# Counts before ranks, and comparisons in half precision, at the end of a routing stage

## The chip, the core and the metric

The kernel runs on one core of one Trainium2 chip. The metric is the device time of one execution in microseconds; before the change it is 438.07 us, the median of 3 runs (436.51 to 440.91). A core has five engines that run their own instruction streams and meet at semaphores: TensorE (PE, matmuls), VectorE (DVE), ScalarE (ACT), GpSimd (POOL) and SyncE (SP, which here only issues DMAs). PE's clock has two levels, 1.2 and 2.4 GHz, and the profile shows which was granted.

## The reference

A block of a transformer with two gated parts. `x` has 4 x 1024 rows of 256; the context has 77 rows of 256 for each of the 4 sequences.

```
h  = layernorm(x)
s  = h @ ctx^T / 16,  masked where query and key are both past the length
x1 = x + tanh(g_x) * (softmax(s) @ ctx @ W^T + b)

h2      = layernorm(x1)
routing = softmax(h2 @ router^T)              # 8 experts
top 2 of 8, their weights normalised to sum 1
y_e     = (silu(h2 @ Wg_e^T) * (h2 @ Wu_e^T)) @ Wd_e^T      # hidden 512
out     = x1 + tanh(g_f) * sum over the 2 chosen experts of weight * y_e
```

Each of the 4096 rows goes to 2 of 8 experts, so there are 8192 (row, expert) entries. The kernel computes an expert only for the rows that chose it.

## The kernel before, in words

**Stage one** (to about 100 us) goes over the rows in 8 groups of 512 (GROUPS = 8, 4 tiles of 128 rows each). Per group: scores, softmax and attention on PE, ACT and DVE; the row sums; the router's logits; then on DVE the two largest of 8 logits for each row and their one-hot form `oh` (L903). POOL adds the two to `picks` (L464), keeps running counts per expert (`carry`), normalises the rows and writes them with their 8 combining weights to `pay`. SP stores `pay` to `xn_rows` in HBM (L333), 512 rows at a time, and also the sums to the output, and between these it issues the loads of the experts' weights `raw` (L327), all in one queue and in order.

**The list.** The second stage needs, for each expert, the list of its rows, padded to whole pairs of 128-row tiles: 78 columns (TILES) of 128 places, 39 pairs (PAIRS). It is built without sorting. PE gives each entry its rank within its expert by products with a triangular matrix (`ranks`, L1112 to L1116), and the counts of all experts (L1151, L1153). A unit is one choice of one tile, so there are 64 units (UNITS) of 128 entries, 8 (CU) for a group. For an entry, the low 7 bits of its rank say the place within a column, and the start of its expert plus the high bits say the column. DVE writes two one-hot forms for each unit: `at_low` (L801, 128 x 128 in float16, which also carries the row's number), and `at_tile` (L949, the column's one-hot form, 78 wide, done for 16 units (CHUNK) in one comparison). PE then adds `at_low[u]^T @ at_tile[u]` over the 64 units (L1163), and the result is the list. Five small steps of DVE (L955 to L963) turn it into `idx`.

**The end of stage one on DVE** (function around L903 to L949), in order: oh of the last group; at_low of the group before, 8 units; the share of the last group; its ranks (po, rank), their low and high bits (low_i, high, low); then, once PE has the counts, nti, nts, ntf, cum, start (the rounded counts and their running sum), starts (start times oh, over all 64 units), first (its sum over 8 experts), col (first plus high). Each of these eight waits for the one before it, and one at_low of the last group stands behind each as a filler. Then four comparisons for at_tile. `mark` adds a semaphore step to an instruction and `after` waits for it.

**PE meanwhile** runs products that nobody reads (`keep_busy`, L1030: 128 x 512 in bfloat16, 22 of them before the counts, 18 behind the ranks and 22 behind the list).

**Stage two** takes the pairs in order. POOL gathers the 2 x 128 rows of a pair by `idx` from `xn_rows` (L495), four pairs ahead; before the first gather it waits for idx, for all stores of `xn_rows` and of the sums. PE transposes them (L1213 for the first pair, L1173 later), ACT and DVE cut them into a high and a low part (`xtT`), and three products stand for one in float32: gate and up (L1182), then down (L1203). ACT and DVE cut the weights of the next pair the same way (`gu`, `dn`). POOL adds the results to the output (L503). SP waits for the first gathers before it loads experts 4 to 7.

Of the kernel before, what the change touches and what calls it, by code (L numbers as in the profile page):

```python
# [14 lines left out]
P = 128  # L15
# [40 lines left out]
def moe_flamingo(nc, x, xT, ctx_rows, ctxT, lens, g_x, g_f, w_rows, wT, b_row, b_col, router, weights, out):  # L56
# [3 lines left out]
    with es:  # L60
        def sb(name, shape, dt=F32, stack=es):
            return stack.enter_context(nc.sbuf_tensor(name, shape, dt))
# [4 lines left out]
        def sem(name):  # L67
            return es.enter_context(nc.semaphore(name))
# [39 lines left out]
        iota_t = sb("iota_t", [P, TILES], F16, a)  # L108
# [25 lines left out]
        oh = sb("oh", [P, GROUPS, TOPK, G, NE], F32, a)  # L134
# [15 lines left out]
        starts = sb("starts", [P, UNITS, NE], F32, a)  # L150
        first = sb("first", [P, UNITS], F32, a)
        col = sb("col", [P, UNITS], F32, a)
# [9 lines left out]
        start = sb("start", [P, NE], F32, a)  # L162
# [6 lines left out]
        at_tile = sb("at_tile", [P, UNITS, TILES], F16, a)  # L169
# [71 lines left out]
        counts_ready = sem("counts_ready")  # L241
        tile_hot = sem("tile_hot")
# [164 lines left out]
        def _(pool):  # L407
# [30 lines left out]
            gp.iota(iota_t[:], [[1, TILES]], base=0, channel_multiplier=0, **exact)  # L438
# [3 lines left out]
            gp.dma_start(out[N:N + P, :], pad_tile[:, 0:D]).then_inc(y_added, Y_ADDED0)  # L442
            pool.wait_ge(gates_ready, 1)
# [248 lines left out]
        def _(dve):  # L692
# [18 lines left out]
            def mark(ins):  # L711
                steps[0] += 1
                ins.then_inc(dve_steps, 1)
                return steps[0]
# [55 lines left out]
            def share(k):  # L770
                dve.wait_ge(gap_sum_ready, k + 1)
                v.reciprocal(rw[:], ed1[:]).then_inc(share_ready, 1)
# [21 lines left out]
            def at_lows(k, units):  # L794

                if k < 0:
                    return
                dve.wait_ge(places_ready, k + 1)
                for u in units:
                    n = k * G + u % G  # L800
                    last = ts(at_low[:, k * CU + u], iota_p[:], low[:, k * CU + u:k * CU + u + 1], code[:, n:n + 1],  # L801
                              ALU.is_equal, ALU.mult)
                if u == CU - 1:
                    last.then_inc(low_ready, 1)
# [34 lines left out]
            for k in range(GROUPS):  # L839
# [66 lines left out]
                if more:  # L906
                    inverted = reciprocal_sums(n)
                elif k == GROUPS - 1:
                    at_lows(k - 1, range(CU))
                if k < 2:  # L910
                    values(k + 2)

            last_group = GROUPS - 1
            share(last_group)
            dve.wait_ge(chosen, GROUPS)
            ranked = unit_ranks(last_group, own_ranks(last_group))
# [3 lines left out]
            dve.wait_ge(counts_ready, 1)  # L920
            counted = mark(ts(nti[:], L[:, COUNTS:COUNTS + NE], float(PT - 1), None, ALU.add))
            at_lows(last_group, range(0, 1))
            after(counted)

            counted = mark(ts(nts[:], nti[:], PT.bit_length() - 1, 1, ALU.logical_shift_right, ALU.logical_shift_left))
            at_lows(last_group, range(1, 2))
            after(counted)
            counted = mark(v.tensor_copy(ntf[:], nts[:]))
            at_lows(last_group, range(2, 3))
            after(counted)  # L930
            counted = mark(v.tensor_tensor_scan(cum[:], one8[:], ntf[:], 0.0, ALU.mult, ALU.add))
            at_lows(last_group, range(3, 4))
            after(counted)
            begun = mark(tt(out=start[:], in0=cum[:], in1=ntf[:], op=ALU.subtract))
            at_lows(last_group, range(4, 5))
            after(begun)
            begun = mark(tt(out=starts[:], in0=oh[:].rearrange("p g c t e -> p (g c t) e"),
                            in1=start[:].unsqueeze(1).to_broadcast([P, UNITS, NE]), op=ALU.mult))
            at_lows(last_group, range(5, 6))
            after(begun)  # L940
            begun = mark(v.tensor_reduce(first[:], starts[:], axis=AX.X, op=ALU.add))
            at_lows(last_group, range(6, 7))
            after(begun)
            after(high_bits)
            begun = mark(tt(out=col[:], in0=first[:], in1=high[:], op=ALU.add))
            at_lows(last_group, range(7, 8))
            after(begun)
            for c in range(0, UNITS, CHUNK):
                tt(out=at_tile[:, c:c + CHUNK], in0=iota_t[:].unsqueeze(1).to_broadcast([P, CHUNK, TILES]),  # L949
                   in1=col[:, c:c + CHUNK].unsqueeze(2).to_broadcast([P, CHUNK, TILES]),  # L950
                   op=ALU.is_equal).then_inc(tile_hot, 1)
# [72 lines left out]
        def _(pe):  # L1024
# [133 lines left out]
            for u in range(UNITS):  # L1158
                if u % CHUNK == 0:
                    pe.wait_ge(tile_hot, u // CHUNK + 1)  # L1160
                if u % CU == 0:
                    pe.wait_ge(low_ready, u // CU + 1)
                last = mm(L[:, LIST:LIST + TILES], at_low[:, u], at_tile[:, u], start=(u == 0), stop=(u == UNITS - 1))  # L1163
            last.then_inc(list_ready, 1)
            keep_busy(22)
# [48 lines left out]
            last.then_inc(xT_ready, 1)  # L1214
            pe.wait_ge(x_low, 1)
# [59 lines left out]
```

## Time and profile before

| | before |
|---|---|
| median of 3 runs | 438.07 us |
| lowest, highest | 436.51, 440.91 us |
| the profiled execution's own time | 438.52 us |
| its span in the trace | 436.7 us |
| PE busy | 413.7 us, 95% |
| DVE busy | 314.8 us, 72% |
| ACT busy | 285.4 us, 65% |
| POOL busy | 251.4 us, 58% |
| mean granted PE clock | 0.979 |

The span is what the trace covers; the execution's time is 1.8 us more. PE's share of busy time is high in part because the unread products count as work. The profile divides the span into 40 slices of 10.9 us; the slice in tenths of each engine:

```profile
PE   8999889967899999999999999999999999999991
DVE  4448999994476777767767777777776777777771
POOL 5015446434236665766676665676667676567664
PEclk9999999988799999999999999999999999999997
```

Each digit is a tenth of full; PEclk is the granted clock. Slices 9 to 11 (87 to 120 us) are the passage from stage one to stage two, which the change is about.

### The profile page before, as it was taken

What the parts mean: (1) busy time and instruction counts of PE and PEld (TensorE: products, weight loads), DVE (VectorE), ACT (ScalarE), POOL (GpSimd) and SP (SyncE); (2) the same over time, 40 slices, a digit from 0 to 9 for tenths busy, and PEclk for the clock granted to TensorE, in tenths of its full rate; (3) what the DMA queues carried; (4) which work ended last, traced back from release to release, by engine and by line L of the source; (5) the groups of instructions that cost most, each with busy time, mean ns of one, the idle gap of its engine ahead of it and who ended that gap; (6) DMA issues with size and microseconds to landing.
All of it is one profiled execution on the core that took longest, in us unless ns stands there. A gap on an engine that the chain in (4) does not pass through costs nothing.

```text
span 436.7 us, 9843 instructions
## 1 busy us (share of the span) xinstructions
PE 413.7 (95%) x3237; PEld 378.9 (87%) x3237; DVE 314.8 (72%) x707; ACT 285.4 (65%) x581; POOL 251.4 (58%) x271
## 2 busy tenths in 40 slices
PE   8999889967899999999999999999999999999991
PEld 3778665534799999999999999999999999999991
DVE  4448999994476777767767777777776777777771
ACT  2698786302377767677676776767767677676770
POOL 5015446434236665766676665676667676567664
PEclk9999999988799999999999999999999999999997
DMA  6956866777457775434333343333433334333343
GB/s 196 328 181 210 267 211 207 248 245 235 109 141 162 162 162 138 67 59 69 50 56 57 59 72 49 54 58 60 66 55 53 56 61 68 55 52 58 63 64 65
DMA packets 34720, 50.52 MB, mean 116 GB/s; under 512 B 3878, under 2 KB 26055, under 8 KB 34695
## 3 DMA queue, kind: packets, MB, share of 16 engines
q0 software_dynamic: 13536, 19.46, 27.2%
q1 hardware_dynamic: 19815, 29.84, 22.2%
q10 hardware_dynamic: 1344, 0.92, 0.7%
q8 instruction: 11, 0.18, 0.2%
q14 instruction: 14, 0.11, 0.1%
HBM read 32.51 MB, written 17.70 MB: 115 GB/s over the span
## 4 chain that ended last, share of the span: by engine, by line
PE 75%; DVE 7%; DMA 7%; ACT 4%; issue 3%; POOL 2%; ACTq 1%; POOLq 0%; DVEq 0%
PE GT L1182 21%; PE Y L1203 20%; PE UP L1182 20%; DMA out_rows<-y,idx 4%; PE W L1030 3%; PE XT L1173 3%; DMA brow<-in_b_row 2%; DVE at_low L801 2%; PE O L1105 2%; ACT ex L582 2%; PE S L1055 2%; POOL xt L495 1%; DVE at_tile L949 1%; ACTq L538 1%; DMA xt<-xn_rows,idx 1%
## 5 line engine op out<-in xcount | busy, mean ns | idle before, releaser
L503 POOL DMA_INDIRECT out_rows<-y,idx x68 | 114.3, 1681 | 97.3 <-ACT y L654 66.6
L973 DVE TENSOR_TENSOR gu<-raw,gu 128x1024 fp32r<-128x1024 f32 x70 | 85.8, 1226 | 65.1 <-ACT gu L630 62.3
L1182 PE MATMUL GT<-xtT,gu 128*128 128x256 f32 x828 | 114.5, 288 | 2.6 <-DVE xtT L973 1.4
L495 POOL DMA_INDIRECT xt<-xn_rows,idx x76 | 97.1, 1277 | 33.7 <-issue 22.9
L1182 PE MATMUL UP<-xtT,gu 128*128 128x256 f32 x828 | 111.2, 284 | 0.0
L1182 PEld LDWEIGHTS GT<-xtT,gu 128*128 128x128 f32 x828 | 104.7, 193 | 4.6 <-DVE xtT L973 1.8
L1182 PEld LDWEIGHTS UP<-xtT,gu 128*128 128x128 f32 x828 | 105.0, 193 | 0.0
L1203 PE MATMUL Y<-dn,hT 128*128 128x256 f32 x816 | 103.5, 283 | 0.0
L1203 PEld LDWEIGHTS Y<-dn,hT 128*128 128x128 f32 x816 | 100.4, 192 | 0.0
L630 ACT CAST gu<-raw 128x1024 fp32r x68 | 70.8, 1042 | 34.3 <-PE UP L1182 31.9
L994 DVE TENSOR_TENSOR hid<-hid,UP 128x512 f32<-128x512 f32 x68 | 46.5, 684 | 9.3 <-PE UP L1182 9.0
L638 ACT CAST xtT<-XT 128x512 fp32r<-128x512 f32 x36 | 21.1, 587 | 42.4 <-issue 25.6
L973 DVE TENSOR_TENSOR hT<-hid,hT 128x512 fp32r<-128x512 f32 x68 | 46.6, 685 | 0.8
L643 ACT ACTIVATE hid<-GT 128x512 f32<-128x512 f32 x69 | 41.0, 594 | 9.0 <-PE GT L1182 7.4
L1030 PE MATMUL W<-ones 128*128 128x512 bf16 x180 | 44.0, 395 | 1.1 <-POOL ones L410 1.1
L647 ACT CAST hT<-hid 128x512 fp32r<-128x512 f32 x68 | 42.1, 619 | 3.8 <-DVE hid L994 2.3
L973 DVE TENSOR_TENSOR dn<-raw,dn 128x1024 fp32r<-128x1024 f32 x35 | 42.7, 1219 | 0.1
L654 ACT ACTIVATE y<-Y,xt 128x256 f32<-128x256 f32 x68 | 32.3, 475 | 6.3 <-PE Y L1203 5.4
L1030 PEld LDWEIGHTS W<-ones 128*128 128x128 bf16 x180 | 17.9, 102 | 21.3 <-issue 3.3
L634 ACT CAST dn<-raw 128x1024 fp32r x34 | 35.6, 1048 | 0.0
L973 DVE TENSOR_TENSOR xtT<-XT,xtT 128x512 fp32r<-128x512 f32 x36 | 24.8, 690 | 13.5 <-ACT xtT L638 13.5
L464 POOL TENSOR_TENSOR picks<-oh 128x32 bf16<-128x32 f32 x8 | 2.0, 251 | 46.1 <-DVE oh L903 46.1
(156 smaller groups left out, 382.5 us busy)
## 6 DMA issues: line engine op xcount, KB each, us to landing
raw<-in_weights SPq DMA_DIRECT2D x32, 384.0 KB
xn_rows<-pay SPq DMA_DIRECT2D x8, 528.0 KB, 3.6
xTg<-in_xT SPq DMA_DIRECT2D x8, 512.0 KB, 4.2
xg<-in_x SPq DMA_DIRECT2D x8, 512.0 KB, 6.0
out_rows<-xg SPq DMA_DIRECT2D x8, 512.0 KB, 3.0
xt<-xn_rows,idx POOLq DMA_INDIRECT x76
out_rows<-y,idx POOLq DMA_INDIRECT x68
kr<-in_ctx_rows SPq DMA_DIRECT2D x1, 308.0 KB
```

Source lines behind the costliest of these rows:

```text
L495: gp.indirect_dma_start(out=xt[:, 2 * s + t, :], out_offset=None, in_=xn_rows, in_offset=bass.IndirectOffsetOnAxis(ap=idx[:, 2 * j + t:2 * ...
L503: gp.indirect_dma_start(out=out, out_offset=bass.IndirectOffsetOnAxis(ap=idx[:, 2 * j + t:2 * j + t + 1], axis=0), in_=y[:, j % 2, t, :], ...
L630: nc.scalar.copy(gu[:, 0, q], gate_up_of(e, q)).then_inc(gu_high[q], 1)
L634: nc.scalar.copy(dn[:, 0, b], down_of(e)).then_inc(dn_high, 1)
L643: nc.scalar.activation(hid[:, q].rearrange("p h t -> p (h t)"), GT[:, q], ACT.Silu).then_inc(silu_ready, 1)
L647: nc.scalar.copy(hT[:, 0, 2 * q:2 * q + 2], hid[:, q]).then_inc(hid_high, 1)
L654: nc.scalar.mul(y[:, s % 2, t], Y[:, t, 0:D], xt[:, 2 * s + t, bass.ds(e + CW, 1)]).then_inc(y_ready, 1)
L973: return tt(out=out, in0=whole, in1=high.bitcast(F32), op=ALU.subtract)
L994: tt(out=wide, in0=wide, in1=UP[:, q], op=ALU.mult).then_inc(hid_ready, 1)
L1030: mm(W[:], ones[:], ones[:].unsqueeze(1).to_broadcast([P, G, P]), start=True, stop=True)
L1182: last = mm(bank[:, h * PT:(h + 1) * PT], gu[:, pw, q, c, w, h * P:(h + 1) * P], xtT[:, b, px, c], start=(c == 0 and n == 0), stop=(c == D ...
L1203: last = mm(Y[:, t, 0:D], hT[:, px, 2 * q + c, t * P:(t + 1) * P], dn[:, pw, b, q, c * D:(c + 1) * D], start=(q == 0 and c == 0 and px == ...
```

## The change

It rearranges the end of stage one on DVE. The counts (nti to start) come first, behind four at_low of group 6, with the other four as their fillers. Then po, starts, rank, first, the bits, and col. Three of the four at_tile comparisons follow, then all eight at_low of the last group, then the fourth comparison. `oh`, `start`, `starts` become bfloat16 and `col` float16; `iota_t` is written out for 16 units (78 x 16 instead of 78), and `at_tile` has the units innermost, so that all three operands of a comparison are 16 bits wide and step by one element. PE reads `at_tile` with a step of 16 elements. POOL writes the larger `iota_t` behind its two padding stores. The unread products behind the list go from 22 to 34, and 6 are added behind the first transposes.

```diff
-        iota_t = sb("iota_t", [P, TILES], F16, a)
+        iota_t = sb("iota_t", [P, TILES, CHUNK], F16, a)
-        oh = sb("oh", [P, GROUPS, TOPK, G, NE], F32, a)
+        oh = sb("oh", [P, GROUPS, TOPK, G, NE], BF16, a)
-        starts = sb("starts", [P, UNITS, NE], F32, a)
+        starts = sb("starts", [P, UNITS, NE], BF16, a)
-        col = sb("col", [P, UNITS], F32, a)
+        col = sb("col", [P, UNITS], F16, a)
-        start = sb("start", [P, NE], F32, a)
+        start = sb("start", [P, NE], BF16, a)
-        at_tile = sb("at_tile", [P, UNITS, TILES], F16, a)
+        at_tile = sb("at_tile", [P, UNITS // CHUNK, TILES, CHUNK], F16, a)
...
-            gp.iota(iota_t[:], [[1, TILES]], base=0, channel_multiplier=0, **exact)
             gp.iota(J[:], [[2, PAIRS]], base=0, channel_multiplier=0, **exact).then_inc(pool_consts, 1)
             pool.wait_ge(pool_consts, 4)
             gp.dma_start(xn_rows[N:N + P, :], pad_tile[:]).then_inc(pads_stored, 16)
             gp.dma_start(out[N:N + P, :], pad_tile[:, 0:D]).then_inc(y_added, Y_ADDED0)
+            gp.iota(iota_t[:], [[1, TILES], [0, CHUNK]], base=0, channel_multiplier=0, **exact).then_inc(tile_iota, 1)
...
-                elif k == GROUPS - 1:
-                    at_lows(k - 1, range(CU))
...
+            at_lows(last_group - 1, range(0, 4))
             share(last_group)
+            dve.wait_ge(counts_ready, 1)
+            dve.wait_ge(ranks_ready, GROUPS)
+            counted = mark(ts(nti[:], L[:, COUNTS:COUNTS + NE], float(PT - 1), None, ALU.add))
+            at_lows(last_group - 1, range(4, 5))
+            after(counted)
+            counted = mark(ts(nts[:], nti[:], PT.bit_length() - 1, 1, ALU.logical_shift_right, ALU.logical_shift_left))
+            at_lows(last_group - 1, range(5, 6))
+            after(counted)
+            counted = mark(v.tensor_copy(ntf[:], nts[:]))
+            at_lows(last_group - 1, range(6, 7))
+            after(counted)
+            counted = mark(v.tensor_tensor_scan(cum[:], one8[:], ntf[:], 0.0, ALU.mult, ALU.add))
+            at_lows(last_group - 1, range(7, 8))
+            after(counted)
+            begun = mark(tt(out=start[:], in0=cum[:], in1=ntf[:], op=ALU.subtract))
             dve.wait_ge(chosen, GROUPS)
-            ranked = unit_ranks(last_group, own_ranks(last_group))
+            own = own_ranks(last_group)
+            after(begun)
+            begun = mark(tt(out=starts[:], in0=oh[:].rearrange("p g c t e -> p (g c t) e"),
+                            in1=start[:].unsqueeze(1).to_broadcast([P, UNITS, NE]), op=ALU.mult))
+            ranked = unit_ranks(last_group, own)
+            after(begun)
+            begun = mark(v.tensor_reduce(first[:], starts[:], axis=AX.X, op=ALU.add))
             masked = low_bits(last_group, ranked)
             high_bits = mark(v.tensor_single_scalar(high[:], rank[:], P.bit_length() - 1, ALU.logical_shift_right))
             low_places(last_group, masked)
-            dve.wait_ge(counts_ready, 1)
-            counted = mark(ts(nti[:], L[:, COUNTS:COUNTS + NE], float(PT - 1), None, ALU.add))
-            at_lows(last_group, range(0, 1))
-            after(counted)
-            counted = mark(ts(nts[:], nti[:], PT.bit_length() - 1, 1, ALU.logical_shift_right, ALU.logical_shift_left))
-            at_lows(last_group, range(1, 2))
-            after(counted)
-            counted = mark(v.tensor_copy(ntf[:], nts[:]))
-            at_lows(last_group, range(2, 3))
-            after(counted)
-            counted = mark(v.tensor_tensor_scan(cum[:], one8[:], ntf[:], 0.0, ALU.mult, ALU.add))
-            at_lows(last_group, range(3, 4))
-            after(counted)
-            begun = mark(tt(out=start[:], in0=cum[:], in1=ntf[:], op=ALU.subtract))
-            at_lows(last_group, range(4, 5))
-            after(begun)
-            begun = mark(tt(out=starts[:], in0=oh[:].rearrange("p g c t e -> p (g c t) e"),
-                            in1=start[:].unsqueeze(1).to_broadcast([P, UNITS, NE]), op=ALU.mult))
-            at_lows(last_group, range(5, 6))
-            after(begun)
-            begun = mark(v.tensor_reduce(first[:], starts[:], axis=AX.X, op=ALU.add))
-            at_lows(last_group, range(6, 7))
             after(begun)
             after(high_bits)
-            begun = mark(tt(out=col[:], in0=first[:], in1=high[:], op=ALU.add))
-            at_lows(last_group, range(7, 8))
-            after(begun)
-            for c in range(0, UNITS, CHUNK):
-                tt(out=at_tile[:, c:c + CHUNK], in0=iota_t[:].unsqueeze(1).to_broadcast([P, CHUNK, TILES]),
-                   in1=col[:, c:c + CHUNK].unsqueeze(2).to_broadcast([P, CHUNK, TILES]),
+            after(mark(tt(out=col[:], in0=first[:], in1=high[:], op=ALU.add)))
+            dve.wait_ge(tile_iota, 1)
+            for c in range(UNITS // CHUNK):
+                if c == UNITS // CHUNK - 1:
+                    at_lows(last_group, range(CU))
+                tt(out=at_tile[:, c], in0=iota_t[:],
+                   in1=col[:, c * CHUNK:(c + 1) * CHUNK].unsqueeze(1).to_broadcast([P, TILES, CHUNK]),
                    op=ALU.is_equal).then_inc(tile_hot, 1)
...
-                last = mm(L[:, LIST:LIST + TILES], at_low[:, u], at_tile[:, u], start=(u == 0), stop=(u == UNITS - 1))
+                last = mm(L[:, LIST:LIST + TILES], at_low[:, u], at_tile[:, u // CHUNK, :, u % CHUNK], start=(u == 0), stop=(u == UNITS - 1))
             last.then_inc(list_ready, 1)
-            keep_busy(22)
+            keep_busy(34)
...
             last.then_inc(xT_ready, 1)
+            keep_busy(6)
             pe.wait_ge(x_low, 1)
             gate(0, 0, 0)
```

## Rows read from the trace of the kernel before

**Rows 1.** The chain of waits, 84 to 112 us: start, us, what it was.

```profile
87.48 0.87 DVE at_low L801 x4
...
91.68 0.22 DVE at_low L801
...
92.20 0.60 DVE starts L937
...
94.20 5.48 DVE at_tile L949 x4
...
99.73 1.23 PE L L1163 x16
...
100.98 0.24 DVE sign L955
...
102.35 1.09 POOL xt L495
...
103.75 4.38 DMA xt<-xn_rows,idx
...
108.18 1.13 PE XT L1213 x4
```

**Rows 2.** The chain of waits from 108 us on, the same columns.

```profile
110.69 2.93 PE GT L1182 x12
113.62 2.01 PE UP L1182 x12
...
126.53 1.44 PE GT L1182 x12
...
129.41 0.44 PE XT L1173 x4
```

**Rows 3.** The sync queue in order of time: start, us, queue, line, what, count.

```profile
85.85 7.39 SPq L327 DMA_DIRECT2D raw<-in_weights  x6
93.28 0.43 SPq L333 DMA_DIRECT2D xn_rows<-pay  x1
99.73 3.31 SPq L327 DMA_DIRECT2D raw<-in_weights  x4
```

**Rows 4.** DMA issues: size, us to landing; whole run, then 90 to 94.

```profile
xn_rows<-pay SPq DMA_DIRECT2D x8, 528.0 KB, 3.6
...
xn_rows<-pay SPq DMA_DIRECT2D x1, 528.0 KB, 8.0
```

**Rows 5.** POOL in order of time: start, us, line, what [idle before, releaser].

```profile
4.65 0.23 POOL L437 IOTA iota_p<- 128x128 f16 x1
...
31.31 0.25 POOL L464 TENSOR_TENSOR picks<-oh 128x32 bf16<-128x32 f32 x1 [24.30 <-DVE oh L903]
...
91.30 0.25 POOL L483 TENSOR_TENSOR pay<-cw 128x32 f32<-128x32 f32 x1
```

**Rows 6.** PE in order of time, 78 to 112 us, the unread products.

```profile
88.13 4.04 PE L1030 MATMUL W<-ones 128*128 128x512 bf16 x18
...
100.75 5.12 PE L1030 MATMUL W<-ones 128*128 128x512 bf16 x22
```

**Rows 7.** Windows: length, busy PE, PEld, DVE, ACT, POOL; clock, DMA share, GB/s.

```profile
94.00:95.00 1.00, 0.00 (x0) 0.00 (x0) 1.00 (x2) 0.00 (x0) 0.00 (x0) 0.67 1.04 412
...
105.00:106.00 1.00, 0.87 (x5) 0.20 (x2) 0.29 (x1) 1.00 (x2) 0.94 (x1) 1.00 0.97 350
...
107.00:108.00 1.00, 0.00 (x0) 0.00 (x0) 0.00 (x0) 0.45 (x1) 0.75 (x1) 0.99 0.29 106
...
114.00:115.00 1.00, 1.00 (x8) 1.00 (x7) 0.00 (x0) 0.00 (x0) 0.00 (x0) 0.59 0.03 8
```

**Rows 8.** DVE in order of time, the kr steps of the start.

```profile
8.61 0.33 DVE L726 TENSOR_SCALAR kr<-kr,kmv 85x256 f32<-85x256 f32 x1
...
9.20 0.88 DVE L732 TENSOR_SCALAR kr<-kr,kmv 85x256 f32<-85x256 f32 x3
```

**Rows 9.** The chain of waits, 0 to 60 us: one stretch of xg.

```profile
41.96 0.78 DVE xg L846 x2
```

More of the change, by code:

```diff
@@ L241, in moe_flamingo @@
         counts_ready = sem("counts_ready")
+        tile_iota = sem("tile_iota")
         tile_hot = sem("tile_hot")
```

## The prediction

> **What bounds the kernel now.** I read the chain of waits first. It is one line of work through the end of stage one: DVE alone from 87.5 to 99.7 us (at_low rows, the small steps from rank to col, then four at_tile comparisons in 5.48 us), the last 16 list products (1.23), five DVE steps to idx, the first gathers, the transposes, then matmuls [rows 1]. From about 125 us to the end PE matmuls follow each other without a gap, so what moves the first gate matmul moves the end by as much [rows 2]. The reader should see in rows 1 that the weak spot is wide: 23 us pass between the last choice of experts (87.48) and the first gate matmul (110.69).
>
> Then I read what else reaches the first gather, which the chain does not show. POOL waits there for idx, but also for the normalised rows of the last group to be stored in HBM. The sync queue issues that store at 93.28, behind six weight loads that take it 7.39 us to issue, and the issue table gives 8.0 us from issue to landing, against a median of 3.6 over all eight such stores [rows 3, 4]. So it lands at 93.28 + 8.0 = 101.28 (counted from the end of its issue, 101.7), and the first gather starts at 102.35. **The store is only 0.6 to 1.1 us behind idx.** Nothing in the change touches it: POOL finished those rows at 91.30 + 0.25, before the queue had issued the loads in front [rows 3, 5].
>
> Last I read PE's clock by the microsecond. The fillers ahead of the list end at 88.13 + 4.04 = 92.17, and the granted clock falls from 2.4 to 1.2 GHz during 94 to 95 (0.67). It is up again behind the list. The fillers there end at 100.75 + 5.12 = 105.87, PE stands idle for 2.31, the clock falls just before 108 (0.99 in that slice), and it is back only during 114 to 115 (0.59) [rows 6, 7]. So the first transposes, gate and up products run at half clock: 1.13, 2.93 and 2.01 us, where later ones take 0.44, 1.44 and 1.44 [rows 1, 2].
>
> **The change, part by part.** *Order.* Sixteen at_low rows lay between oh and the first at_tile; now eight do, and the other eight stand before the last at_tile. An at_low takes 0.22 on the chain, and some take more, say 0.23 [rows 1]: the first at_tile comes 8 x 0.23 = 1.85 earlier, the last none. The count steps had at_low rows as fillers and keep them; first, low and col now wait for one another. Most of these steps have another one between themselves and what they wait for, so I put 0.0 here; at the range's end one exposed step of the size of sign, 0.24 [rows 1].
>
> *Widths.* A comparison has 1248 columns and takes 1.37 from start to start, about 1.04 ns a column and 0.07 besides [rows 1]. All its operands are now 16 bits wide and run along memory. No row of before shows a two-input operation in that form, so the ends are: unchanged, 1.37; or the rate of a faster kind, the one-input kr step, (0.88 - 0.33) / 2 = 0.275 for 256 columns, where the two-input xg takes 0.78 / 2 = 0.39 [rows 8, 9]. That is 0.45 ns a column less, 0.59, so 1248 x 0.59 + 0.07 = 0.8. I take 0.8, since nothing but the width changes. The Trainium skill (VectorE: DVE Perf Modes, What auto-detection actually checks) says that an operation on two tensors handles two values a cycle if every tensor is 16-bit with step 1; by it the comparison would take 0.72, and the trace neither shows nor denies it. Likewise starts falls from 0.60 to 0.37; first, po, oh and picks keep their width on one side and cost what they did.
>
> *Sum on DVE.* First at_tile: 94.20 - 1.85 - 0.23 = 92.1. Three of them, 2.4: 94.5. Eight at_low, 1.85: 96.4. The last, 0.87: 97.2, against 99.68. The last 16 products at half clock, 1.23: 98.5; from there to the first gather 102.35 - 100.98 = 1.37 [rows 1]. By DVE alone the gather would start at 99.8, 2.5 us earlier. **But the store lands at 101.28**, and POOL needed 0.28 from idx to the gather, so I put the start at 101.5: a gain of 0.85, the rest is given back to the wait for the store.
>
> *Gathers.* Pair 0 landed 4.38 after its second gather's issue, while the four loads issued from 99.73 kept the DMA engines full to 106 (share 0.97 in the last slice) [rows 1, 3, 7]. These loads wait for earlier loads, not for DVE, so they stay, and an earlier gather runs more of its time against them. Of 0.85 I keep 0.7 (ends: 0.3, and all).
>
> *List products.* at_tile is now read with 16 values between neighbours. In the kernel before the last 16 took 1.23 us, 77 ns each at half clock, and 48 of 64 were hidden behind comparisons [rows 1]. Here the first comes at 93.0, and 48 products have until 97.2: 87 ns each. Unchanged cost is covered; what a slow read would do is a rival below.
>
> *Fillers.* 34 instead of 22 behind the list. 18 fillers take 4.04, 0.22 each [rows 6]. PE has idled only from 92.17 to 93.0 this time, then about 2 us before the last 16 products, so the clock may still be full: the list ends at 97.9 and the fillers at 97.9 + 7.5 = 105.4; at half clock it ends at 98.5 and some seven fillers take double, 107.5. Pair 0 lands at about 107.4. Six more fillers, 1.3, lie in the 1.38 that PE waits for xtT, 108.18 + 1.13 to 110.69 [rows 1, 2]. Cost on the path nothing; if the clock is low they take 2.6 and push the gate product by 1.2. What they buy: transposes, gate and up at full clock, 6.07 - (0.44 + 2 x 1.44) = **2.75 us** [rows 1, 2].
>
> *The rest.* iota_t grows to 1248 columns and moves behind two DMA issues on POOL. The 128 columns of iota_p take 0.23; at that rate iota_t takes 2.2, and POOL stands idle for the 24.30 before 31.31 [rows 5]. The two issues (padding rows) come 0.2 earlier, and nobody waits for them before 100 us. DVE gets two new waits: for iota_t, long written, and for the last ranks ahead of the count steps. PE issues counts and ranks in front of the fillers of 88.13 [rows 6]; DVE comes to the wait at 87.48 + 0.87 + 0.2 = 88.6, so nothing queues behind it. oh in bf16 changes only the width of what POOL's picks reads (0.25), not its count [rows 5].
>
> *Together:* 0.7 + 2.75 = 3.4 us off the profiled execution's 438.52 (span 436.7 and 1.8 around it), which is 0.45 above the median of 438.07. I forecast **434.7**.
>
> **Rivals.** *The clock falls again (0.27).* It fell 2.1 to 2.2 us after PE stopped, both times [rows 6, 7]. If the list runs at full clock the fillers end at 105.4 and 2.0 us stay open: a coin's toss. Then the products run low again, and the six fillers cost 1.2 but bring the clock back sooner: I give this 1.0 instead of 2.75: 438.1 - 0.7 - 1.0 = 436.4. For it: the gap is nearly the old one. Against: any lateness of the list closes it.
>
> *The store is not the end of the wait (0.17).* If its landing as the queue shows it is not what POOL waits for, or it lands sooner, the full 2.5 of DVE counts, and 2.75 of the clock at best: 438.1 - 5.2 = 432.9. Against: the 8.0 us, and the loads that share the engines.
>
> *The comparisons are no faster (0.10).* Then the last ends at 92.1 + 4.1 + 1.85 + 1.44 = 99.5, as before; the list ends at 100.3, and the fillers at 107.7, just past the gather. The gate gets its clock, less 0.5: 436.0.
>
> *The strided read (0.06), slower.* The chain decides for it when the list ends later than 100.98: 64 products from 93.0, so above 125 ns each, 1.6 times the 77 of the half clock. At four times, 260 ns, the list ends at 109.6 and the kernel is 8.6 slower: 446.7. The matmul rows give no sign of it; nothing in the kernel before reads a strided moving operand in 16 bits. The Trainium skill (Advanced Engine Details and Errata, Memory Cachelines) says that SBUF has lines of 16 bytes and that an access which changes line each time pays; here neighbours lie 32 bytes apart, so by that rule every column pays an amount that the page does not give. Up to 1.6 times it is hidden, as worked out above.
>
> The forecast itself has 0.40.
>
> **The numbers.** What a measurement of this kernel tells from no change is about 1%, 4.4 us. 433.7 is reached only by the second rival and by the forecast with all of the gather's gain and a lucky execution: 0.24 faster. Slower than 442.4 asks for the strided read: 0.05. The rest, 0.71, is within. The range takes in the forecast, the low clock and the store's rival: 432.4 to 437.8.
>
> **What would show it.** In the profile of the changed kernel: at_tile near 0.9 each, the last ending at 97; idx at 99 to 100, but the first gather not before 101.3, with POOL idle after idx; granted clock 1.00 from 108 to 112, and the first gate and up at 1.44 each. Wrong: a gather at 100, which ends my store; transposes at half clock; or list products above 100 ns at the full clock.

## The result and the profile after

The changed kernel takes **441.16 us**, the median of 22 runs (438.58 to 444.52), against 437.73 for the kernel before in the same comparison (22 runs). The ratio is 1.0079 with a 95% interval of [1.0057, 1.0101]: slower by 3.4 us, where I forecast 3.4 us faster. The profiled execution took 444.52 us (span 442.7), the longest of the 22, and so 6.0 us more than the profiled one of before; part of that is this execution's own, as shown below. Medians are over all executions; where some of an experiment's were disturbed (e4, e7, e9, e10, e11), its ratio rests on the undisturbed ones alone.

The chain of waits of the changed kernel, 84 to 125 us (start, us, what it was). It answers to [rows 1, 2].

```profile
89.43 0.23 DVE oh L905
...
92.42 0.41 DVE starts L937
...
94.15 0.82 DVE at_tile L952
...
95.01 9.31 PE L L1166 x64
104.32 9.34 PE W L1033 x34
113.65 0.45 PE XT L1216 x4
...
115.49 1.70 PE GT L1185 x12
117.19 1.44 PE UP L1185 x12
```

The reader should see that DVE's part did what it was to do: from the start of oh to the first at_tile 4.7 us. But from 95.01 there is one block, 64 list products in 9.31 us, 145 ns each, where the kernel before hid 48 of 64 and showed 16 at 77 ns. Behind it stand the 34 fillers, 9.34 us, and the transposes start the moment that they end.

The comparisons and the products by tile, after (engine, operation, count: duration in ns min/median/max, first and last start).

```profile
L1166 PE MATMUL L<-at_tile,at_low x64: 301/323/324, 95.0 to 104.0; 128*128 128x78 f16 x64
L952 DVE TENSOR_TENSOR at_tile<-iota_t,col x4: 797/800/807, 94.1 to 98.1; 128x1248 f16<-128x1248 f16 x4
```

(One product lasts longer than 145 ns since the next starts before it has ended.) Three of the four comparisons were done at 96.4, the last at 98.9, and DVE then waited 5.5 us for the list. The windows of one us around the fall of PE's clock (columns as in [rows 7]; the first busy figure is PE with its count), and the products that run at or behind 98.0:

```profile
96.00:97.00 1.00, 1.00 (x10) 0.82 (x8) 1.00 (x5) 0.00 (x0) 0.00 (x0) 1.00 1.05 396
97.00:98.00 1.00, 1.00 (x10) 0.82 (x8) 1.00 (x6) 0.00 (x0) 0.00 (x0) 1.00 0.98 325
98.00:99.00 1.00, 1.00 (x10) 0.89 (x8) 0.89 (x2) 0.00 (x0) 0.00 (x0) 0.50 0.97 212
99.00:100.00 1.00, 1.00 (x10) 0.89 (x8) 0.00 (x0) 0.00 (x0) 0.00 (x0) 0.50 0.90 330
```

```profile
L1166 PE MATMUL L<-at_tile,at_low x45: 322/323/324, 97.7 to 104.0; 128*128 128x78 f16 x45
```

The counts take in the products that cross an edge of their window; the rate is read from the starts. The first 19 of the 64 lie between 95.01 and 97.7, 142 ns from start to start, at a granted clock of 1.00; the other 45 start between 97.7 and 104.0, 143 ns apart, nearly all at 0.50. So the clock is not what makes them slow. It fell in the middle of them, 3.0 us behind the first, though the records show PE busy all that time. In front of the first PE had stood idle for 0.67 us; e1 and e12 below have the same gap (0.60 and 0.66) and kept the full clock.

The store and the gathers after: the sync queue, then POOL.

```profile
95.25 0.43 SPq L335 DMA_DIRECT2D xn_rows<-pay  x1
...
105.73 1.11 POOL L497 DMA_INDIRECT xt<-xn_rows,idx  x1 [11.72 <-DVE idx L966]
```

Counted from the issue of this store, which the change does not move, the first gather starts 10.48 us later; before it was 102.35 - 93.28 = 9.07 [rows 1, 3]. The list alone costs 1.4 us. The transposes start at + 18.40, before at + 14.90: 3.5. The first gate product starts at + 20.24 (before + 17.41), and the first up product ends at 118.63 - 95.25 = 23.38 (before 115.63 - 93.28 = 22.35 [rows 2]): between the two the full clock gave 2.5 us back, 0.7 at the transposes and 1.8 in the first gate and up products, and what stays is 1.0.

The other 5.0 us of the profiled difference lie elsewhere. The last group's oh starts at 89.43 instead of 87.25, because in this execution the clock fell once in the group loop; the windows of the changed kernel, then of the kernel before:

```profile
50.00:52.00 2.00, 2.00 (x12) 2.00 (x12) 1.39 (x7) 2.00 (x8) 2.00 (x4) 0.55 0.52 183
52.00:54.00 2.00, 2.00 (x13) 1.09 (x12) 0.65 (x3) 0.19 (x2) 1.14 (x5) 0.59 0.65 230
```

```profile
50.00:52.00 2.00, 2.00 (x20) 1.52 (x20) 1.57 (x8) 1.72 (x8) 1.92 (x5) 1.00 0.68 231
52.00:54.00 2.00, 2.00 (x16) 1.84 (x14) 1.91 (x12) 0.52 (x3) 0.74 (x3) 1.00 0.50 180
```

That is 2.0 us on the store's issue (95.25 against 93.28), and the code that runs there is that of before except for the narrower `oh`. The traces of e1, e4, e9 and e12 below show one such fall too, all between 22 and 27 us; those of before and of the other eight don't. All five with it have the change's front, but five with that front (e2, e5, e7, e8, e10) lack it, so whether the change has to do with it is open. The rest, 3.0 us, is behind the first pair: PE waits there for gathered rows, which it never did in the trace of before (who waited for whom from 112 us on: total us, times, longest):

```profile
PE XT L1176 <- DMA xt<-xn_rows,idx: 2.4, 3, 1.3
```

### The profile page after: what moved, and what is told of

Read it like the earlier page. It is cut to its first block, busy times and chain, and to the rows that moved or that the text cites. A ratio compares the mean times of both kernels' runs of the same rounds, so it can differ in the third digit from the quotient of the medians.

```text
span 442.7 us, 9881 instructions
## 1 busy us (share of the span) xinstructions
PE 423.7 (96%) x3255; PEld 384.2 (87%) x3255; DVE 312.5 (71%) x707; ACT 285.4 (64%) x581; POOL 255.8 (58%) x271
## 4 chain that ended last, share of the span: by engine, by line
PE 66%; DMA 12%; DVE 6%; issue 6%; ACT 5%; POOL 3%; POOLq 0%; ACTq 0%; DVEq 0%; SPq 0%
PE GT L1185 17%; PE Y L1206 16%; PE UP L1185 16%; DMA out_rows<-y,idx 10%; PE W L1033 5%; PE XT L1176 3%; PE S L1058 2%; PE L L1166 2%; PE O L1108 2%; ACT ex L584 2%; POOL xt L497 2%; DVE at_low L803 2%; DMA kr<-in_ctx_rows 1%; ACT squares L561 1%; POOL out_rows L505 1%
## 5 line engine op out<-in xcount | busy, mean ns | idle before, releaser
L505 POOL DMA_INDIRECT out_rows<-y,idx x68 | 118.8, 1748 | 97.2 <-ACT y L656 61.8
L497 POOL DMA_INDIRECT xt<-xn_rows,idx x76 | 95.3, 1254 | 34.6 <-issue 22.6
L1185 PE MATMUL GT<-xtT,gu 128*128 128x256 f32 x828 | 113.3, 286 | 1.3 <-ACT hid L645 1.1
L1185 PEld LDWEIGHTS GT<-xtT,gu 128*128 128x128 f32 x828 | 103.6, 191 | 3.3 <-ACT hid L645 1.4
L1033 PE MATMUL W<-ones 128*128 128x512 bf16 x198 | 50.6, 409 | 1.1 <-POOL ones L412 1.1
L1033 PEld LDWEIGHTS W<-ones 128*128 128x128 bf16 x198 | 20.5, 105 | 24.9 <-issue 6.3
L466 POOL TENSOR_TENSOR picks<-oh 128x32 bf16<-128x32 bf16 x8 | 2.0, 244 | 46.4 <-DVE oh L905 46.4
```

The source lines that it names most:

```text
L497: gp.indirect_dma_start(out=xt[:, 2 * s + t, :], out_offset=None, in_=xn_rows, in_offset=bass.IndirectOffsetOnAxis(ap=idx[:, 2 * j + t:2 * ...
L505: gp.indirect_dma_start(out=out, out_offset=bass.IndirectOffsetOnAxis(ap=idx[:, 2 * j + t:2 * j + t + 1], axis=0), in_=y[:, j % 2, t, :], ...
L1033: mm(W[:], ones[:], ones[:].unsqueeze(1).to_broadcast([P, G, P]), start=True, stop=True)
L1185: last = mm(bank[:, h * PT:(h + 1) * PT], gu[:, pw, q, c, w, h * P:(h + 1) * P], xtT[:, b, px, c], start=(c == 0 and n == 0), stop=(c == D ...
```

## The experiments

Theory A: a list product costs by the distance in memory between the values that PE reads. Theory B: the products are slow through the clock, or through DVE and the DMAs at work beside them, or the order or types are to blame. Theory C: once the list is fast, the first gather waits for the store of the last rows. Theory D: what an earlier entry into stage two gains is given back later, because PE comes to pairs whose rows the weight loads have delayed. The fillers are priced on their own.

**Units innermost two at a time** (e1_inner2): all as changed, but neighbours 4 bytes apart.

```diff
-        at_tile = sb("at_tile", [P, UNITS // CHUNK, TILES, CHUNK], F16, a)
+        at_tile = sb("at_tile", [P, UNITS // 2, TILES, 2], F16, a)
...
-                tt(out=at_tile[:, c], in0=iota_t[:],
-                   in1=col[:, c * CHUNK:(c + 1) * CHUNK].unsqueeze(1).to_broadcast([P, TILES, CHUNK]),
+                wide = [P, CHUNK // 2, TILES, 2]
+                tt(out=at_tile[:, c * CHUNK // 2:(c + 1) * CHUNK // 2], in0=iota_t[:].unsqueeze(1).to_broadcast(wide),
+                   in1=col[:, c * CHUNK:(c + 1) * CHUNK].rearrange("p (g i) -> p g i", i=2).unsqueeze(2).to_broadcast(wide),
```

> The changed kernel with the units innermost two at a time instead of sixteen: neighbours that PE reads lie 4 bytes apart instead of 32, and the comparison keeps 16-bit operands that step by one. Theory A (what a list product costs is set by the distance between the values it reads): the products fall from 145 ns to between 35 (full clock) and 80 (half clock), the comparison stays at 0.80, the list ends within 1.3 us of the last comparison, the first gather starts at the store's landing or a little after the list (0.6 to 3 us earlier than before the change), and the time is 434 to 436.5 against 437.7 before. Theory B (the products are slow because of the clock that fell at 98 us, or because DVE and the DMAs use the memory at the same time): still 120 ns or more each, and a time above 439.

436.19 us, ratio to before 0.9977 [0.9945, 1.0008]. PE in order of time:

```profile
94.17 2.21 PE L1167 MATMUL L<-at_tile,at_low 128*128 128x78 f16 x48 [0.60 <-DVE at_tile L953]
98.11 0.77 PE L1167 MATMUL L<-at_tile,at_low 128*128 128x78 f16 x16 [1.73 <-DVE at_tile L953]
98.73 7.50 PE L1034 MATMUL W<-ones 128*128 128x512 bf16 x34
108.47 0.66 PE L1217 MATMUL XT<-ident,xt 128*128 128x128 f32 x4 [2.24 <-DMA xt<-xn_rows,idx]
```

48 products take 2.21 us, 46 ns each, and the comparisons keep their 801 ns. Same clock (1.00), same order, similar DMA traffic (busy share 0.88 to 0.98, against 0.98 to 1.05 at 96 to 98 us of the changed kernel): theory B falls, A stands. Against the changed kernel this is 1.0% or 4.5 us. The chain of waits also shows what takes over once the list is quick:

```profile
94.62 7.13 DMA xn_rows<-pay
...
102.00 0.83 issue
102.83 1.10 POOL xt L497
...
104.23 4.19 DMA xt<-xn_rows,idx
```

idx is ready at 100.0, and the first gather waits until 102.83 for the store of the last rows, which takes 7.13 us to land; POOL adds 1.08 from the landing to the gather, of which 0.83 is issue. From the store's issue to the gather it is now 8.21 instead of 9.07 us.

**Units outermost again** (e2_units_outer): the order, types and fillers of the change with the layout of before.

```diff
-                tt(out=at_tile[:, c], in0=iota_t[:],
-                   in1=col[:, c * CHUNK:(c + 1) * CHUNK].unsqueeze(1).to_broadcast([P, TILES, CHUNK]),
+                tt(out=at_tile[:, c * CHUNK:(c + 1) * CHUNK], in0=iota_t[:].unsqueeze(1).to_broadcast([P, CHUNK, TILES]),
+                   in1=col[:, c * CHUNK:(c + 1) * CHUNK].unsqueeze(2).to_broadcast([P, CHUNK, TILES]),
```

> The changed kernel with at_tile in the layout of before (units outermost) and the column, in float16, repeated along the innermost dimension; order, fillers and the other types stay as changed. Theory A: products at 77 ns or less as before, comparisons back at 1.37 though all operands are 16 bits wide; the last comparison ends 2.3 us later than the changed kernel's 98.9, the list some 1.3 later, about 102.5 at the changed kernel's scale, against 104.3: 1.8 us gained on the changed kernel, of which fillers may hold back a part: 438 to 440. Theory B: products at 120 ns or more, 440 to 443. If the 16-bit types alone make the comparison fast, it stays at 0.80.

437.84 us, ratio 1.0024 [0.9995, 1.0053], just below the 438 to 440 that I expected. The comparisons, and PE:

```profile
L952 DVE TENSOR_TENSOR at_tile<-iota_t,col x4: 1451/1452/1458, 91.7 to 97.6; 128x1248 f16<-128x1248 f16 x4
...
93.19 0.76 PE L1166 MATMUL L<-at_tile,at_low 128*128 128x78 f16 x16 [1.31 <-DVE at_tile L952]
...
99.08 1.22 PE L1166 MATMUL L<-at_tile,at_low 128*128 128x78 f16 x16 [1.93 <-DVE at_tile L952]
```

Products at 0.76 / 16 = 48 ns at the full clock and 1.22 / 16 = 76 at half; comparisons back at 1452 ns, though all three operands are 16 bits wide. So the narrow types alone bring nothing; the operand that is repeated along the innermost dimension keeps the slow rate.

**The stride alone** (e3_stride_alone), in the kernel before:

```diff
-                tt(out=at_tile[:, c:c + CHUNK], in0=iota_t[:].unsqueeze(1).to_broadcast([P, CHUNK, TILES]),
+                tt(out=at_tile[:, c // CHUNK].rearrange("p t u -> p u t"), in0=iota_t[:].unsqueeze(1).to_broadcast([P, CHUNK, TILES]),
...
-                last = mm(L[:, LIST:LIST + TILES], at_low[:, u], at_tile[:, u], start=(u == 0), stop=(u == UNITS - 1))
+                last = mm(L[:, LIST:LIST + TILES], at_low[:, u], at_tile[:, u // CHUNK, :, u % CHUNK], start=(u == 0), stop=(u == UNITS - 1))
```

> The kernel before with one edit: at_tile has the units innermost, sixteen at a time, DVE writes it so (float32 column, as before) and PE reads it with a distance of 32 bytes. Order, types and fillers are those of before. Theory A: 145 ns a product; from 95.6 the 64 take 9.3 us, the list ends at 104.9 instead of 101.0, and the kernel is 3.5 to 4.2 us slower than before: 441.2 to 442. Theory B (order, types or fillers are to blame): products at 77 ns, time as before within 1 us.

453.26 us, ratio 1.0385 [1.0332, 1.0439]: far more than I expected, for a reason that I had left out. By tile, and PE:

```profile
L949 DVE TENSOR_TENSOR at_tile<-iota_t,col x4: 5370/5615/5620, 94.2 to 109.7; 128x1248 f16<-128x1248 f16 x4
...
115.39 2.44 PE L1163 MATMUL L<-at_tile,at_low 128*128 128x78 f16 x16 [2.80 <-DVE at_tile L949]
```

DVE now writes at a distance of 32 bytes, and a comparison takes 5.6 us instead of 1.45. The products are 2.44 / 16 = 153 ns, at half clock, in the order and with the types of before (more than 145 since the end of the last counts for more among 16): that half confirms A. As a measurement of the read's price in time this kernel is spoilt, since DVE bounds it.

**The distance in steps** (e8_inner8, e12_inner4): as e1_inner2 with eight units innermost, 16 bytes, and with four, 8 bytes; one execution each.

> As e1_inner2 with the units innermost eight at a time: neighbours 16 bytes apart. If what costs is the distance in 16-byte lines, a product takes the 145 ns of 32 bytes (each value in another line); if it grows evenly with the distance, between 46 and 145, about 85. The comparison stays at 0.80.

> As e1_inner2 with the units innermost four at a time: neighbours 8 bytes apart, two in each 16 bytes. 4 bytes gave 46 ns a product, 16 bytes 143, 32 bytes 145. If a new 16-byte line for every value is what costs, 8 bytes stay near 46 to 50; if each doubling of the distance costs until one value comes out of each line, 70 to 80.

The list products of the first kernel, and of the second:

```profile
92.66 9.14 PE L1167 MATMUL L<-at_tile,at_low 128*128 128x78 f16 x64 [0.67 <-DVE at_tile L953]
```

```profile
94.81 3.65 PE L1167 MATMUL L<-at_tile,at_low 128*128 128x78 f16 x48 [0.66 <-DVE at_tile L953]
```

| distance | a product | where |
|---|---|---|
| 2 bytes | 48 ns | e2, full clock |
| 4 bytes | 2.21 / 48 = 46 ns | e1 |
| 8 bytes | 3.65 / 48 = 76 ns | e12 |
| 16 bytes | 9.14 / 64 = 143 ns | e8 |
| 32 bytes | 9.31 / 64 = 145 ns | changed kernel |

The price grows 1.65 and 1.9 times with the steps to 8 and to 16 bytes and stops there, which is the second of the two forecasts for e12. In e8 too the clock fell within the block and the products kept their rate. The Trainium skill (Advanced Engine Details and Errata, Memory Cachelines) has lines of 16 bytes in SBUF and a penalty when every access meets another line; by that rule the trace agrees at 16 and 32 bytes. The whole kernels took 440.68 (e8) and 437.35 (e12). The page also says that at least two hits on a line are needed to absorb the latency of an access; two were not enough here: at 8 bytes, two values in each 16, a product still costs 1.65 times the 46 ns.

**22 fillers instead of 34** (e4_fillers22), in the changed kernel:

```diff
-            keep_busy(34)
+            keep_busy(22)
```

> The changed kernel with 22 unread products behind the list as before, instead of 34; the six behind the transposes stay. Theory A with fillers as a second cost: in the changed kernel the transposes start when the 34 fillers end (113.65), though pair 0's rows landed near 111; so 22 fillers bring the transposes 2 us earlier, and the time goes from 441.2 to about 439.2, unless PE's clock falls again, then 440.5. If the rows landed only at 113.5 (fillers hide under the gather), the time stays at 441.2 within 0.5.

438.15 us, ratio 1.0025 [0.9994, 1.0057], 0.54% or 2.4 us below the changed kernel. The chain:

```profile
103.60 7.09 PE W L1033 x22
110.69 0.45 PE XT L1216 x4
...
112.53 1.69 PE GT L1185 x12
```

From the end of the list to the transposes 7.09 us instead of 9.34, and the clock was at 1.00 for the gate product (1.69). Here too the transposes follow the last filler at once, so the rows had landed by then; the twelve more were pure delay.

**The fillers alone** (e6_fillers_alone), in the kernel before: 34 behind the list, 6 behind the transposes.

```diff
-            keep_busy(22)
+            keep_busy(34)
...
             last.then_inc(xT_ready, 1)
+            keep_busy(6)
```

> The kernel before with only the fillers of the change: 34 unread products behind the list, 6 behind the first transposes. My prediction priced this at 2.75 us gained (first transposes, gate and up at the full clock): 434.5. The fillers there would end at 108.45, 0.3 after the rows land. If the clock is worth less on the chain, 436 to 437; if the fillers hold up the transposes, above 437.

437.83 us, ratio 1.0011 [0.9983, 1.0040]: nothing. Its trace shows the gain on the spot. The transposes, and PE's first gate and up products:

```profile
107.65 0.45 PE XT L1213 x4
...
109.48 1.70 PE L1182 MATMUL GT<-xtT,gu 128*128 128x256 f32 x12
111.03 1.60 PE L1182 MATMUL UP<-xtT,gu 128*128 128x256 f32 x12
```

From the start of the transposes to the end of up 111.03 + 1.60 - 107.65 = 5.0 us, against 115.63 - 108.18 = 7.45 before. So 2.5 us of my 2.75 are in this execution, and none in the median. One trace can't say in how many executions of the kernel before the clock falls there; where it does not, the fillers have nothing to give. One more trace shows that it need not: e11 below, whose code up to there is that of the kernel before, with its 22 fillers. There the clock was low until 104 us (0.50 at 103 to 104, 0.91 in the next), the fillers behind the list took longer (6.46 us against 5.12), and the transposes followed them at once:

```profile
107.31 0.45 PE XT L1214 x4
...
109.14 1.69 PE GT L1183 x12
110.84 1.44 PE UP L1183 x12
```

That is 5.0 us again from the transposes to the end of up, without an added filler. A hint that this is common: over the span, the mean granted clock of the kernel before lay between 0.976 and 0.990 in the executions timed beside these experiments, those at 0.990 took 435.0 to 435.4 us and those at 0.976 some 438 to 440, and the profiled one had 0.979. How common was not counted. A rival is untested: in e6 the transposes start the moment that the 34 fillers end, 5.93 us behind the first gather (101.72), in e11 5.06 us behind it (102.25), so the twelve more may also have held them up.

**The store first** (e5_store_first): e1_inner2 with one swap in the sync queue.

```diff
-            load_weights(2, range(PARTS))
             store_xn(GROUPS - 1)
+            load_weights(2, range(PARTS))
```

> The kernel with units innermost two at a time (fast comparison, fast read), and the store of the last normalised rows ahead of the four loads of expert 2 in the sync queue. Theory C (with a fast list the first gather waits for that store): the store lands 3 us or more earlier, near 97 to 98, the gather follows idx at about 100.3 instead of 102.8, and the transposes move from 108.5 to 106 or 107; time 1.5 to 2.5 us below the kernel without it: 433.7 to 434.7. Rival (the first gathers are held by the weight loads anyway, which run to 106): the gather is issued earlier but lands where it did, time 436.2 as without it.

435.39 us, ratio 0.9956 [0.9930, 0.9982]. The gathers on the chain of waits, and who waited behind 112 us:

```profile
98.62 1.09 POOL xt L497
...
100.02 5.40 DMA xt<-xn_rows,idx
...
105.63 0.66 PE XT L1217 x4
...
PE XT L1177 <- DMA xt<-xn_rows,idx: 1.9, 1, 1.9
```

The store is issued at 91.51 and lands 3.9 us later; the gather follows idx by 0.3 us, at 98.62. Theory C is shown. The rival has a part: the second gather's rows take 5.40 us to land instead of 4.19. Counted from the start of the last group's oh, since e1's lies 1.7 us later (88.60 against 86.91), the transposes come after 105.63 - 86.91 = 18.7 us, in e1 after 108.47 - 88.60 = 19.9: 1.15 us earlier, and PE then waits 1.9 us for a later pair. The ratios of e1 and e5 differ by 0.2%, 0.9 us, and their intervals overlap, so what the swap gives in time is not clear of noise.

**The loads behind the gathers** (e7_loads_behind): also the loads of experts 2 and 3 behind the first four pairs' gathers, and 24 fillers.

```diff
             store_xn(GROUPS - 1)
-            load_weights(3, range(PARTS))
             for s in range(AHEAD):
                 sp.wait_ge(tile_loaded[s], 32)
+            load_weights(2, range(PARTS))
+            load_weights(3, range(PARTS))
```

> As e5_store_first, and the loads of experts 2 and 3 (3 MB) issued only when the first four pairs' rows have landed; 24 fillers behind the list instead of 34. If the loads hold up the first gathers, pair 0 lands 3 us after its second gather's issue instead of 4.2, near 104.6, and with 24 fillers (to about 104) the transposes start there: 431 to 432.5. If they do not, 433.7 to 434.7 as e5. If expert 2 comes too late (its first pair is ten pairs in, about 190 us), ACT waits for it and the time is 438 or more.

435.90 us, ratio 0.9944 [0.9914, 0.9974]. The transposes start at 103.18, 2.4 us before those of e5 (2.8 when both are counted from oh), and the time shows little of it (0.9944 against 0.9956, intervals that overlap):

```profile
103.18 0.66 PE L1217 MATMUL XT<-ident,xt 128*128 128x128 f32 x4 [0.44 <-DMA xt<-xn_rows,idx]
...
PE XT L1177 <- DMA xt<-xn_rows,idx: 6.0, 5, 2.0
```

The traced execution took 438.81 us, 2.9 above the median of e7, so 6.0 us of waits may be more than its usual.

**Paced loads** (e9_store_paced, e10_all_paced, e11_before_paced): the parts of later experts issued one behind the gather of each pair, in e5, in e7 (from expert 2 on), and in the kernel before. The edit of e9:

```diff
             for e in range(4, NE):
                 for part in range(PARTS):
+                    j = PARTS * e + part - 12
+                    sp.wait_ge(tile_loaded[j % XR], 32 * (j // XR + 1))
                     sp.wait_ge(raw_loaded, 16 * (PARTS * e + part))
```

> e5_store_first plus one edit: the sync queue loads the 16 parts of experts 4 to 7 one behind the gather of each pair from the fifth on, instead of back to back. Theory D (an earlier entry into stage two is given back later, because PE comes to a pair whose rows have not landed: POOL issues that gather behind a scatter-add, which waits for the landing of the scatter-add before it, and the weight loads beside them make the landings slow): the waits of PE for xt behind 125 us vanish (1.9 us in e5), the DMA share falls there, and the time is 1 to 2 us below e5's 435.4: 433.5 to 434.5. Rival (the scatter-adds are slow by themselves): waits and time stay as in e5, 435.4.

> e7_loads_behind with all loads from expert 2 on issued behind the gathers of the pairs: two parts a pair for experts 2 and 3, one a pair for 4 to 7; 24 fillers. Theory D: the entry stays at 103.2 us as in e7, PE's 6.0 us of waits for xt behind 125 us vanish, and the time is 430.5 to 432. Rival: 435 to 436 as e7. If an expert's weights come too late, ACT waits for raw and it is above 437.

> The kernel before with only the paced loads of experts 4 to 7. Its trace shows no wait of PE for xt behind 125 us, so theory D expects nothing, within 0.5 us of 437.6 (fewer slow executions at the most). If the pacing gains as much here as in e9, it is a gain of its own and says nothing on what an early entry loses.

Ratios 0.9964 [0.9913, 1.0014], 0.9914 [0.9888, 0.9940] and 1.0048 [1.0022, 1.0073]. Seven of e10's fourteen executions took 431.6 to 436.0 us and seven 440.9 to 444.9; e9's seven took 433.5, 433.8, 439.0 and four times 440.5 to 444.0. Over all executions the medians (438.43 and 440.50) lie above the 436.85 of before, so neither is a version to take. PE from 200 to 300 us (columns as in [rows 7]) in the kernel before and in e11, and what PE waits for in e11 behind 112 us:

```profile
200.00:300.00 100.00, 100.00 (x837) 99.67 (x837) 74.30 (x89) 71.27 (x110) 66.80 (x45) 1.00 0.37 59
```

```profile
200.00:300.00 100.00, 97.95 (x814) 96.93 (x813) 72.04 (x85) 69.37 (x108) 64.31 (x43) 1.00 0.47 91
```

```profile
PE XT L1174 <- DMA xt<-xn_rows,idx: 2.0, 4, 0.6
```

In e11 the loads now lie beside these pairs, and PE loses 2.0 of the 100 us, all of it in waits for gathered rows; in the kernel before it loses none. The time agrees: 0.48% is 2.1 us. So half of theory D holds: loads beside the gathers delay rows that PE waits for. The other half, that spreading the loads cures it, was not borne out: e11 is slower than before where I expected nothing, and e9 and e10 show no gain over all their executions. That spread-out loads meet more pairs is my reading and was not tested by itself.

## Why the prediction was wrong

**List products: the step that failed.** I took the price of a product as unchanged ("unchanged cost is covered") and gave the strided read 0.06. It costs 145 ns, above the 125 from which I had said that it decides, and at both levels of the clock. The 64 products no longer hide behind the comparisons (9.31 us on the chain), and undoing the distance alone gives 4.5 us back (e1). My rival had the place and the point of decision right and the size wrong: 260 ns and 8.6 us against 145 ns. It was meant as a multiple of the half clock's 77 ns (and four times 77 would have been 308, not 260), but the price of the strided read does not depend on the clock.

**The widths**: right. 0.80 long, (2.25 - 0.80) / 2 = 0.73 from start to start; my bound from rows gave 0.8. By the rule of the Trainium skill that the prediction cites (VectorE: DVE Perf Modes, What auto-detection actually checks) the estimate is 0.72; the trace agrees. starts takes 0.41, I said 0.37. e2 shows that the layout, not the type, earns it: the gain on DVE and the loss on PE were bought with the same edit, and a distance of two units has the one without the other.

**The order and the sum on DVE**: right. From the start of oh to the first at_tile 4.72 us (94.15 - 89.43); by my sum 92.1 - 87.25 = 4.85.

**The store**: right that it is the next end of the wait (e1, e5), and hidden in the changed kernel, where the list is later than the store. The size was luck. I took the landing as unchanged, 8.0 us, and let POOL add 0.2 behind it: 8.2 from issue to gather. In e1 the store landed after 7.13 and POOL added 1.08, in e12 7.07 and 1.07: 8.21 and 8.14. With 1.07 behind the landing, the kernel before was already at this bound: 101.28 + 1.07 = 102.35, where its gather started (the list's end gives the same 102.35, so the trace does not tell the two apart). What I read as slack of the store, 0.6 to 1.1 us, were by this POOL's own steps; with the landing unchanged an earlier list alone would have gained nothing, and the 0.86 us of e1 (9.07 to 8.21) are what its store landed sooner. Why it did is open.

**Fillers**: wrong as forecast. I let 34 end with the rows' landing. With the list late and the clock low they took 9.34 us instead of 7.5, and ended at least 9.34 - 7.09 = 2.25 us after the landing, since with 22 of them the rows were there 7.09 us behind the list (e4). That is 2.4 us of the time.

**The clock**: right on the chain (2.5 of 2.75 us, e6; the first gate product takes 1.70 at the full clock, where I put 1.44), wrong in time (0.1% slower, interval to both sides). I priced it from the one execution that was profiled; in e11 the code of before has the full clock there with its own 22 fillers.

**The remainder.** 1.4 us by the list and 2.1 by the fillers are 3.5 at the transposes, 2.5 is won back by the clock, 1.0 stays, and PE's waits for later gathers (2.4 us in the profiled execution) are added: 3.4. The medians are 3.4 apart as well, but that the two agree proves little, since these waits and the clock differ from execution to execution. The waits are 0 in e1 and e4 and 6.0 us in e7, which enters stage two earliest of the unpaced ones; beyond that I have no rule for them.

## What to carry to other kernels

An edit of a layout that makes one engine faster must be priced on every engine that reads it, and a moving operand whose neighbours lie 8 bytes or more apart is to be measured, not assumed. Look for the layout that both like: units in pairs kept DVE's 0.80 us and PE's 46 ns. When a chain is shortened, list beforehand every other thing that its end waits for, here a store behind four loads in a queue, and move that too: the version with paired units and the store first (e5) is faster than both kernels, 0.9956 [0.9930, 0.9982] of the time of before.

## What was not expected of the hardware

- A matmul with 78 moving columns in float16 takes 46, 76, 143 and 145 ns at 4, 8, 16 and 32 bytes between neighbours, the last two at either level of the clock.
- Such products don't hold the clock. At 16 or 32 bytes it fell within the block 3.0 us (changed kernel), 3.7 us (e4) and 5.0 us (e8) behind the first product, PE busy throughout; at 4 and 8 bytes (e1, e12), behind the same idle gap of 0.6 to 0.7 us, it stayed at 1.00. Whether the slow read itself is the reason was not tested apart.
- DVE's writes at a distance of 32 bytes with operands that are not all 16-bit take 5.6 us for 1248 columns, 4.5 ns each, against 1.45 us; with two units innermost (e1), which DVE writes without gaps and PE reads 4 bytes apart, both are at their fast rate.
- The granted clock can fall once in the group loop, at 50 to 54 us in the changed kernel's trace and at 22 to 27 us in those of e1, e4, e9 and e12. The last group's oh then starts at 88.6 to 89.4 instead of 86.8 to 87.3 us: about 2 us.
